# A decoder layer on one core: x1 copied by DMA, finished tiles moved among residuals, an opening in one DMA queue, and three vectors loaded as rows

## The reference

```python
x = ln(x + attn(x))      # attn: Xn = ln(x)*gamma + beta; Q,K,V = split(Xn @ W_in + b_in)
                         #  K, V = rotary(K), rotary(V)   (first 256 columns, interleaved pairs)
                         #  A = sum over tokens of K/|K| * V/|V|;  A = 0.5*A + 0.5
                         #  (A * Q) @ W_out + b_out + x   -> the sum inside ln is 2x + half_bo terms
x = ln(x + cross(x, ctx, mask))   # fake-quantise x and ctx to fp8 (one scale each: 448/amax), x_q @ ctx_q + mask
x = ln(x + ffn(x))       # silu(x@gate)*(x@up) @ down, plus 8 of 1024 experts per token (product keys, gather)
```

## Time and profile before

| | |
|---|---|
| runs, median | 787.38 us |
| profiled execution | 787.22 us |
| its span | 785.4 us |
| TensorE busy | 98% of the span |
| VectorE busy | 85% |
| GpSimd busy | 47% |
| ScalarE busy | 41% |

### The profile page before, as it was taken

One profiled execution on the slowest core, in us unless ns is written; L12 is line 12 of the kernel. 1 busy time (PEld: TensorE's weight loads), 2 busy tenths in 40 slices (PEclk: granted clock), 3 DMA queues, 4 the chain that ended last, 5 costly groups with the idle time before them and its releaser, 6 DMA issues.

```text
span 785.4 us, 10678 instructions
## 1 busy us (share of the span) xinstructions
PE 768.9 (98%) x3574; PEld 633.6 (81%) x3578; DVE 665.4 (85%) x1348; ACT 321.6 (41%) x700; POOL 371.5 (47%) x324
## 2 busy tenths in 40 slices
PE   8999999999899999999999999999999999999997
PEld 7888887888677878888888888888888888888885
DVE  6889799998799870566689998999999999899876
ACT  6454355455664422232533433334333343344224
POOL 1242332442123311024466776766776677676324
PEclk9999999999999999999999999999999999999999
DMA  8666513715355548001222221421333224242014
GB/s 321 245 128 167 93 55 94 182 23 95 75 135 134 135 115 261 1 1 32 68 72 76 77 92 40 135 86 46 95 117 104 85 79 120 61 130 58 16 54 160
DMA packets 51190, 79.78 MB, mean 102 GB/s; under 512 B 17503, under 2 KB 26335, under 8 KB 50624
## 3 DMA queue, kind: packets, MB, share of 16 engines
q0 software_dynamic: 24240, 31.52, 18.4%
q1 hardware_dynamic: 25312, 47.59, 17.5%
q10 hardware_dynamic: 1584, 0.01, 0.1%
HBM read 110.50 MB, written 12.58 MB: 157 GB/s over the span
## 4 chain that ended last, share of the span: by engine, by line
PE 69%; DVE 2%; issue 1%; ACT 1%; POOL 0%; POOLq 0%; ACTq 0%; DVEq 0%
PE gu L1919 15%; PE gu L1920 15%; PE gu L1921 15%; PE ob L2011 7%; PE ob L2015 7%; PE ob L2010 7%; PE ob L1946 1%; PE ob L2031 1%; PE ob L2027 1%; PE ob L2028 1%; PE gu L1961 0%; PE gu L2131 0%; PE gu L1929 0%; DVE xall L1613 0%; PE gu L1990 0%
## 5 line engine op out<-in xcount | busy, mean ns | idle before, releaser
L1919 PE MATMUL gu<-x_hi,w_hi 128*128 128x512 f32 x504 | 196.6, 390 | 0.0
L1921 PE MATMUL gu<-x_hi,w_lo 128*128 128x512 f32 x504 | 196.1, 389 | 0.0
L1920 PE MATMUL gu<-x_lo,w_hi 128*128 128x512 f32 x504 | 196.1, 389 | 0.0
L1324 POOL TENSOR_TENSOR h_lo<-mid,h_hi 128x512 fp32r<-128x512 f32 x62 | 86.8, 1416 | 172.8 <-ACT h_hi L1479 172.8
L1921 PEld LDWEIGHTS gu<-x_hi,w_lo 128*128 128x128 f32 x504 | 94.6, 188 | 19.8
L1919 PEld LDWEIGHTS gu<-x_hi,w_hi 128*128 128x128 f32 x504 | 94.6, 188 | 19.6
L1920 PEld LDWEIGHTS gu<-x_lo,w_hi 128*128 128x128 f32 x504 | 94.6, 188 | 19.4
L1489 ACT ACTIVATE gates<-dots 128x1 f32<-128x1 f32 x144 | 29.1, 202 | 175.8 <-DVE dots L1752 175.8
L1661 DVE TENSOR_TENSOR mid<-gu,mid 128x512 f32<-128x512 f32 x64 | 43.9, 687 | 65.8 <-PE gu L1921 54.9
L2010 PE MATMUL ob<-w_hi,h_hi 128*128 128x512 f32 x224 | 87.1, 389 | 0.0
L2011 PE MATMUL ob<-w_lo,h_hi 128*128 128x512 f32 x224 | 87.1, 389 | 0.0
(11 more groups left out here) (257 smaller groups left out, 1462.7 us busy)
## 6 DMA issues: line engine op xcount, KB each, us to landing
stage<-in_ctx SPq DMA_DIRECT2D x7, 1024.0 KB, 6.8
total<-prod POOLq DMA_DIRECT2D x11, 384.0 KB, 4.1
xall<-half_bo POOLq DMA_DIRECT2D x4, 1024.0 KB, 9.7
xhat<-in_L_ffn_gate_w SPq DMA_DIRECT2D x8, 512.0 KB, 3.4
xhat<-in_L_ffn_up_w SPq DMA_DIRECT2D x8, 512.0 KB, 3.4
xall<-in_mask_Bx1xS_ff POOLq DMA_DIRECT2D x4, 1024.0 KB, 11.8
xhat<-in_L_ffn_down_w SPq DMA_DIRECT2D x8, 512.0 KB, 3.6
x_dram<-xall SPq DMA_DIRECT2D x4, 1024.0 KB, 7.1
```

The costliest lines, as they stand in the source:

```text
L1324: nc.gpsimd.tensor_tensor(lo[:, c], mid[c][:], hi[:, c].bitcast(F32), ALU.subtract).then_inc(hlo_done, 1)
L1919: nc.tensor.matmul(dst, lhs[0], rhs[0], start=start, stop=False)
L1920: nc.tensor.matmul(dst, lhs[0], rhs[1], start=False, stop=False)
L1921: return nc.tensor.matmul(dst, lhs[1], rhs[0], start=False, stop=stop)
```

## The change

There are seven edits.
- The opening's DMAs all go through SP. x's first half comes in two tiles with a semaphore each, then W_in chunk 0, the identity, and gamma, beta and the query bias as 12 rows of 128 values; chunk 1 now comes ahead of x's second half. The 4 KB of `iota8` come ahead of batch 1's x.
- TensorE transposes the 12 rows into PSUM, and ScalarE copies them into `columns`, ahead of the first `high_w`.
- VectorE's and TensorE's orders in the opening are changed; 13 idle products stand for 16.
- In the third batch two of the four `finish_x1(0, i)` move from ahead of the context's quantisation to places between residuals.
- SP copies the first batch's finished x1 into `stage[0]`. TensorE turns the copy, behind `attention(LAST, i)`, and `add_mask(0)` waits for the copy alone. The wait with 16 fillers behind goes.
- In the last batch `low_ffn`, `multiplier` and `largest_late` change places, and the first attention tile takes chunks 0 to 2 whole and then chunk 3.
- In the second block eight fillers are added ahead of the wait for `y_scaled` and eight behind the first transposes; `middle(0, 1)` goes ahead of `quantise(2, (0,))` and `normalise(1)`.

```diff
-IDLE_PRODUCTS = 16
+IDLE_PRODUCTS = 13
-        def add_mask(b):
-            nc.gpsimd.wait_ge(x1t_mm, TB * (b + 1))
+        def add_mask(b, read=None):
+            nc.gpsimd.wait_ge(*(read or (x1t_mm, TB * (b + 1))))
+            columns = sb("columns", [P, 3 * KC], F32)
+            gam, bet, b_q = (columns[:, r * KC:(r + 1) * KC] for r in range(3))
+            column_rows = prod[0:3 * KC, 0, 0:P]
@@ sync
-                sp.dma_start(xall[:, 0:2 * D], x_tiles[0][:, 0]).then_inc(x_half, 16)
-                sp.dma_start(ident[:], consts[:, C_ID:C_ID + P]).then_inc(ident_in, 16)
+                for i in range(2):
+                    sp.dma_start(xall[:, i * D:(i + 1) * D], x_tiles[0][:, 0, i * D:(i + 1) * D]).then_inc(x_tile[i], 16)
                 for c in range(KC):
                     sp.dma_start(w_stage_of(c), w_in_v[c][:, D:3 * D]).then_inc(w_raw[c], 16)
                     if c == 0:
+                        sp.dma_start(ident[:], consts[:, C_ID:C_ID + P]).then_inc(ident_in, 16)
+                        for r, src in enumerate((gamma, beta, b_in[0:D])):
+                            sp.dma_start(column_rows[r * KC:(r + 1) * KC], src.rearrange("(c p) -> c p", p=P)).then_inc(gb_in, 16)
+                    if c == 1:
                         sp.dma_start(xall[:, 2 * D:4 * D], x_tiles[0][:, 1]).then_inc(x_in[0], 16)
...
                 load_ctx(CTX_ORDER[B - 1])
+                sp.wait_ge(c_quant, B)
+                sp.wait_ge(x1_done, TB)
+                sp.dma_start(stage[0][:], xall[:, 0:TB * D]).then_inc(x1_copied, 16)
@@ gpsimd
-                add_mask(0)
+                add_mask(0, (x1_copied, 16))
@@ scalar
-                for dst, src, count in ((gam, gamma, gb_in), (bet, beta, gb_in), (b_q, b_in[0:D], bq_in)):
-                    act.dma_start(dst[:], src.rearrange("(c p) -> p c", p=P), allow_slow_non_contiguous=True).then_inc(count, 16)
+                act.wait_ge(columns_mm, 1)
+                nc.scalar.activation(columns[:], gu[2][:, 0:3 * KC], ACT.Copy).then_inc(columns_ready, 1)
                 high_w(0)
-                act.wait_ge(gb_in, 32)
+                act.wait_ge(columns_ready, 1)
@@ vector, opening
-                x_stats(0, (0, 1))
+                for i in range(2):
+                    dve.wait_ge(x_tile[i], 16)
+                    x_stats(0, (i,))
                 x_variance(0)
                 normalise(0)
                 low_w(0)
                 low(0, 0)
+                low_w(1)
+                low(0, 1)
                 dve.wait_ge(x_in[0], 16)
                 x_stats(0, (2, 3))
                 x_variance(1)
-                low_w(1)
-                low(0, 1)
+                low_w(2)
+                low(0, 2)
                 normalise(1)
-                for c in range(2, KC):
-                    low_w(c)
-                    low(0, c)
-                for c in range(KC):
-                    low(1, c)
+                low_w(3)
+                low(0, 3)
+                low(1, 0)
+                low(1, 1)
                 dve.wait_ge(bkv_in, 16)
+                add_kv_bias(0, 0)
+                low(1, 2)
+                low(1, 3)
@@ vector, third and last batch
                     if b == 2:
-                        for i in range(TB):
-                            finish_x1(0, i)
+                        finish_x1(0, 0)
+                        finish_x1(0, 1)
                         ctx_quantise(1)
...
+                        else:
+                            finish_x1(0, 2)
                         residual(b - 1, 2)
+                        if b == 2:
+                            finish_x1(0, 3)
                         residual(b - 1, 3)
...
                 last_total()
+                low_ffn(0, gate_s[0])
                 largest_late(0)
+                multiplier(LAST)
                 largest_late(1)
-                multiplier(LAST)
+                low_ffn(1, up_s[0])
                 for c in range(KC):
                     low_y(LAST, c)
-                for s, part in enumerate((gate_s[0], up_s[0])):
-                    low_ffn(s, part)
-                largest_late(2)
-                largest_late(3)
                 residual(LAST, 0)
                 dve.wait_ge(rstd2_ready, LAST)
                 variance((0,))
+                largest_late(2)
                 residual(LAST, 1)
                 variance((1,))
+                largest_late(3)
                 largest_centred(0)
@@ tensor
-                        for k in range(KC):
+                        for chunks in (range(KC),) if b < LAST else (range(KC - 1), (KC - 1,)):
+                            for k in chunks:      # high products, then low products, of these chunks
...
                 pe.wait_ge(ident_in, 16)
+                pe.wait_ge(gb_in, 48)
+                nc.tensor.transpose(gu[2][:, 0:3 * KC], column_rows, ident[0:3 * KC, 0:3 * KC]).then_inc(columns_mm, 1)
                 for c in range(KC):
                     transposes(0, c)
+                pe.wait_ge(columns_ready, 1)
                 for k in range(KC):
-                    if k == 2:
+                    if k == KC - 1:
                         for c in range(KC):
                             transposes(1, c)
...
                         key_value_high(0, i, k)
-                    for i in range(2):
-                        if k:
-                            key_value_low(0, i, k - 1)
+                    if k < KC - 2:
+                        for i in range(2):
+                            key_value_low(0, i, k)
...
-                pe.wait_ge(x1_done, TB)
+                for i in range(TB):
+                    attention(LAST, i)
+                pe.wait_ge(x1_copied, 16)
                 for i in range(TB):
                     pe.wait_ge(kv_out, NT - 1 + i // 2)
                     for c in range(KC):
-                        last = nc.tensor.transpose(gu[i][:, c * P:(c + 1) * P], xall[:, i * D + c * P:i * D + (c + 1) * P], ident[:])
+                        last = nc.tensor.transpose(gu[i][:, c * P:(c + 1) * P], stage[0][:, i * D + c * P:i * D + (c + 1) * P], ident[:])
                     last.then_inc(x1t_mm, 1)
-                for i in range(TB):
-                    attention(LAST, i)
...
-                pe.wait_ge(z_done, NT - 2)
-                keep_running(16)
                 pe.wait_ge(z_done, NT)
                 keep_running(8)
@@ second block, vector
                     variance()
+                    if n == 0:
+                        middle(n, 1)
                     if n + 2 < TB:
                         quantise(n + 2, (0,))
                     normalise(n + 1)
-                    middle(n, 1)
+                    if n:
+                        middle(n, 1)
@@ second block, tensor
+                keep_running(ob[3], 8)
                 pe.wait_ge(y_scaled, 1)
                 keep_running(ob[3], 5)
                 for i in range(2):
                     transposes(1, (i,), own_bank, x1t_mm, freed(y_done, 0))
+                    if i == 0:
+                        keep_running(ob[3], 8)
                     cross(0, nothing, (i,))
```

More of the change, by code:

```diff
@@ L194, in decoder_layer @@
             x_in = [sem(f"x_in{b}") for b in range(B)]
-            x_half = sem("x_half")
+            x_tile = [sem("x_tile0"), sem("x_tile1")]
             w_raw = [sem(f"w_raw{c}") for c in range(KC)]
-            wq_raw, wo_raw = sem("wq_raw"), sem("wo_raw")
-            gb_in, bq_in, bkv_in, hb_in = sem("gb_in"), sem("bq_in"), sem("bkv_in"), sem("hb_in")
+            wq_raw, wo_raw, x1_copied = sem("wq_raw"), sem("wo_raw"), sem("x1_copied")
+            gb_in, columns_mm, columns_ready, bkv_in, hb_in = sem("gb_in"), sem("columns_mm"), sem("columns_ready"), sem("bkv_in"), sem("hb_in")
             c_in, trig_in = sem("c_in"), sem("trig_in")
@@ L261, in _ @@
                 sp.dma_start(qT[:], w_in.rearrange("(c p) n -> p c n", p=P)[:, :, 0:D]).then_inc(wq_raw, 16)
+                sp.dma_start(iota8[:], consts[:, C_IOTA:C_IOTA + TOPK]).then_inc(s_const, 16)
                 load_x(1)
                 sp.dma_start(half_bo[:], b_out.partition_broadcast(P)).then_inc(hb_in, 16)
-                sp.dma_start(iota8[:], consts[:, C_IOTA:C_IOTA + TOPK]).then_inc(s_const, 16)
                 sp.wait_ge(w_lo_done, 2)
@@ L437, in query @@
                         act.wait_ge(wq_lo_done, 1)
-                        act.wait_ge(bq_in, 16)
                     nc.scalar.activation(qT[:, c], ob[2 + c % 2][:], ACT.Identity, bias=b_q[:, c:c + 1]).then_inc(qt_out, 1)
@@ L749, in _ @@
                 nc.vector.memset(kv[:, 1, 1], 0.0).then_inc(idle_ready, 1)
-                dve.wait_ge(x_half, 16)
-                x_stats(0, (0, 1))
+                for i in range(2):
+                    dve.wait_ge(x_tile[i], 16)
+                    x_stats(0, (i,))
                 x_variance(0)
@@ L771, in _ @@
                         ctx_quantise(2)
-                    add_kv_bias(b, 0)
-                    if b == 0:
```

(18 more changed lines are left out.)

4 lines of the change are left out of this document (removed).

## The result

| | before | changed |
|---|---|---|
| median, first set (6 runs each) | 787.45 us (785.88 to 787.59) | 781.18 us (780.13 to 781.68) |
| median, beside the last experiments (9 and 5 runs) | 786.54 us | 781.66 us (781.27 to 781.77) |
| profiled execution: time, span | 787.22, 785.4 | 781.68, 779.9 |

The ratio of the changed kernel's time to that of the kernel before is 0.9927 (95% interval 0.9916 to 0.9937), and 0.9938 (0.9924 to 0.9952) the second time. The forecast was 780.6, the range 778.9 to 783.7. A gain of 6.6 us had been forecast. The medians differ by 6.3 us in the first set and by 4.9 in the second, the two profiled spans by 5.5. Ratios further down are to the kernel before, run beside the kernel in question.

The account below looks back on a forecast made before the run. TensorE, busy 768.9 of 785.4 us, was taken as the bound, with no waits listed from 250 us to the last 6. Terms 1.5 + 1.5 + 1.5 + 1.2 + 0.9 = 6.6 us: 787.22 - 6.6 = 780.6 us, range 778.9 to 783.7.

Parts of the forecast that it names:

- What bounds the kernel: Whole kernel: TensorE, busy 768.9 of 785.4 us; no wait listed from 250 us to the last 6, so earlier gains pass.
- Opening: Up to the first two key/value tiles: faster loads and new orders start tile 2 1.8 us earlier; 1.5 us taken.
- late-rows rival: Opening: rows wait in SP's ring and delay high_w(0); 790.1 us if landing like iota; with other gain-eating costs 7%.
- The second half of the step: Opening, from high_w(0) to tile 2: the new order keeps TensorE fed; 1.2 us of idling goes.
- what VectorE would pass on: Behind the opening: VectorE comes out only some 0.9 us earlier, so 0.3 us is taken off the gain of 1.8.
- Finished tiles: Third batch: two finish_x1 moved among residuals end TensorE's 1.9 us stall; the gain is VectorE's idle time, 1.5 us.
- x1 copy: Last attention products: transposes read a DMA copy and stand behind them, so the last residual comes earlier; 1.5 us.
- the copy does nothing: Last residual: VectorE isn't ready for it, the 1.5 is nil, 782.1 us; VectorE or the copy together 20%.
- Fillers: Join of the two blocks: 8 fillers at each of two waits hold TensorE's clock at 2.4 GHz; 1.2 us.
- middle(0, 1): Second block, near 237 us: run ahead of normalise(1), it ends TensorE's 0.9 us wait for h_lo; 0.9 us.
- the signs named: Trace marks: high_w(0) 6.7 to 7.1, tile 2 near 20.9, stall gone, totals 3 us earlier, clock 1.00, h_lo no releaser.
- VectorE did hold part of the gain: Rival: VectorE limits the opening, stalls between residuals and delays residual(LAST, 3); 782.2 us; VectorE or the copy together 20%.

Follow-up runs that it names:

- the seven traces: Traces of the changed kernel and variants whose changed opening stands unaltered up to the third batch: tile 2 mean 21.71 us, third batch mean 99.31 us.
- the old opening: Everything ahead of the second batch as in the kernel before; put back alone in the changed kernel: 782.27 us, ratio 0.9943.
- batch 0's order: Changed kernel with tile 0's squares ahead of the query weights' copy, batch 1's statistics ahead of tile 0's products, low_wq behind them: 780.59 us, ratio 0.9923.
- the high part first: Changed kernel with ScalarE's high part of W_in chunk 0 ahead of its copy of the 12 columns: 781.48 us, ratio 0.9932.

## Why the prediction was right, and which term was off

**What bounds the kernel.** Right, and the most useful step: no wait is listed behind 250 us, and the last stretch repeats to 0.1 us in twelve kernels. Each us won earlier reached the end.

**Opening: the mis-sized term, 1.5 forecast, 0.3 in the profiled pair and 0.6 over the traces.** It failed in two places. First, high_w(0) was to start 0.6 earlier, at 6.9. The loads came nearly as taken. In the profiled trace the statistics of x's first tile start at 3.36 (3.7 forecast for x) and those of the second at 4.31. By the landings of the DMAs chunk 0 was there at 6.27 to 6.89 in the seven traces, mean 6.62 (6.2 forecast), and at 7.51, 7.84 and 7.67 in the three with the old opening. But the columns' transpose, which was to follow with chunk 0, came 0.3 to 0.9 behind it, mean 0.7, behind the rows (in one trace behind the identity), and high_w(0) stands behind it. In the seven traces high_w(0) starts at 6.99 to 8.09, mean 7.62, and at 7.54, 7.86 and 7.70 with the old opening: 0.1 is won there. That is the late-rows rival at a small scale. The second half of the step held: from high_w(0) to tile 2 13.9 to 14.0 us in five of the seven, 15.2 before, 1.2 won, as forecast. In the other two, 14.2 and 14.7, chunk 1 came late: ScalarE waited 0.62 and 1.08 us for it. Second, what VectorE would pass on. I said that it comes out 0.9 earlier and took 0.3 off. It came out nothing earlier at 26.6, because I followed its own instructions and not ScalarE's: the norms of tile 0 stood behind the query weights' copy, and these behind the moved transposes. That held back 0.6, and not the 0.3 that I took off; the run with batch 0's order gave it back.

**Finished tiles: 1.5 forecast, 1.13 in the pair, 1.3 over the traces.** The stall goes whole and the gain is VectorE's idle time, as argued. Of its 1.1 + 0.4 us the 1.1 goes; the 0.4 for xn_hi stays, which I had counted as won. VectorE's waits of the changed kernel, 97 to 200 us, from the third line of that list on; the first one shown is new, in the last batch, and costs nothing that the stretch to residual(LAST, 3) shows:

```profile
DVE xall L713 <- PE ob L1027: 0.6, 1, 0.6
DVE amax_x L726 <- ACT xall L524: 0.5, 1, 0.5
DVE xn_lo L604 <- ACT xn_hi L421: 0.4, 1, 0.4
```

**x1 copy: 1.5 forecast, 1.7 measured.** Residual(LAST, 3) starts at 198.54, later than the 196.8 to 197.4 named only because the two terms before it were smaller. VectorE followed TensorE at once: the last product starts at 198.11 and lasts 0.39 us. The rival that the copy does nothing is excluded.

**Fillers: 1.2 forecast, 1.6 in the trace, less in the median.** Mechanism right, credit half wrong: by the traces the 8 behind the transposes do it, and those ahead of the wait bring nothing. The size is a matter of the execution, and partly luck: the profiled execution of the kernel before is one in which the clock fell, and in 12 of 31 it seems not to have. The Trainium skill (TensorE: Matmul & The Clock Gate, HAM oscillation) has waits between groups of matmuls as the cause; the runs agree in that, with 1.02 and 1.20 us of waiting and clock 0.51, and with one of the two filled, clock 1.00. But the single waits of the page's example and rule are longer than any of these, and the measurement decides: waits this short can be enough.

**middle(0, 1): 0.9 forecast, 0.8 in the pair, 0.7 by the run without it.** H_hi came at 235.85 behind ScalarE's last magnitude, as stepped through the earlier trace rows: 6.1 earlier than before, 4.7 of it from ahead.

**Sum.** 0.3 + 1.1 + 1.7 + 1.6 + 0.8 = 5.5: the terms that came out larger made up for half of the opening's shortfall. That the median of the first set is only 0.6 off the forecast owes something to luck, since the second set won 1.4 us less; with the terms over the traces and the fillers at 0.1 to 0.6 the sum is 4.4 to 4.9. Of the signs named, the stall, the clock and h_lo came as forecast; high_w(0) and tile 2 were late as said, and the totals' product came 1.4 us earlier (182.94 for 184.36), not 3. VectorE did hold part of the gain, which I gave 20%, but in batch 0 and not between the residuals or at the last one.

## What to carry to other kernels

Where one engine is at 98% and its waits can be counted, cut the span at the places where the parts of a change act, and compare stretches over several traces: here the last three repeat to 0.1 us where total times scatter by 1, while the first two scatter by 0.8 each and need several traces. When work is brought forward, step through each engine that its consumer waits for, here ScalarE's norms behind a copy that could wait. Where a gain depends on whether the clock falls, compare medians, since one trace shows one execution. And a small load that gates the first instruction should not stand behind a large one; nor should the identity that it is transposed with.

## What the runs showed of the hardware that I had not expected

- The same opening lands differently in each execution: rows transposed at 6.65 to 7.78, ScalarE's waits for W_in chunk 1 or 2 up to 1.1 us or none at all, with the same instructions. It is a scatter of 0.8 us at the third batch (98.83 to 99.60).
- A granted clock of 1.2 GHz came after waits of 1.02 and 1.20 us with 1.3 us between them, and not with one wait of 1.02. In another kernel it came after 0.20, 0.33 and 0.56 us at the start of the program, while the changed kernel's 0.82 and 1.14 us there, and 1.69 and 0.56 us with the high part first, left it at 2.4 GHz. The lengths of the waits alone don't decide it; what does stays open.
- Three rows of 2 KB had moved by 4.6 us on a queue with nothing else on it. Behind 1.1 MB in SP's queue the transpose that waits for them came at 6.65 to 7.78 us.
